# Combine step of an attention and mixture-of-experts block: an earlier first load, a second queue, other groups, another order of scales and two norms on VectorE

## The reference

```
x = layernorm(x + attention(x))            # 16 heads of 64, causal, rotary positions
x = layernorm(x + experts(x))              # 16 experts 256 -> 512 -> 256, each token uses 3
layernorm(x) = (x - mean) / sqrt(var + 1e-5)   # over the 256 numbers of a token
```

## Time and profile before

| | us |
|---|---|
| median of three runs | 1894.03 |
| the profiled execution's own time | 1896.07 |
| its span, from the first to the last instruction | 1894.1 |
| last scatter issued by POOL | 1834.14 |
| first load of the combine phase issued | 1840.62 |
| first add of POOL | 1846.17 |
| last norm of ACT ends | 1890.71 |

### The profile page before, as it was taken

One profiled execution on the slowest core, in us unless ns is written; L12 is line 12 of the kernel. 1 busy time (PEld: TensorE's weight loads), 2 busy tenths in 40 slices (PEclk: granted clock), 3 DMA queues, 4 the chain that ended last, 5 costly groups with the idle time before them and its releaser, 6 DMA issues. The chain is left out here.

```text
span 1894.1 us, 33741 instructions
## 1 busy us (share of the span) xinstructions
PE 1727.0 (91%) x9587; PEld 1288.4 (68%) x9588; DVE 1362.5 (72%) x3170; ACT 743.8 (39%) x1583; POOL 1263.0 (67%) x1086
## 2 busy tenths in 40 slices
PE   5389999999999999999999999998679999999970
PEld 4356766766666676667667666754349999999960
DVE  3358888888888888888888888865974544444435
ACT  3124445444445544444444445534442222222213
POOL 2138778767887786787778688833347777777753
PEclk8579999999999999999999999999659999999995
DMA  9856656755665676556657646613944444444447
GB/s 308 283 167 172 174 148 187 211 146 156 187 166 153 197 201 177 168 153 191 180 181 213 164 144 169 177 47 118 374 137 69 71 72 74 73 71 73 72 83 234
DMA packets 184483, 300.41 MB, mean 159 GB/s; under 512 B 22544, under 2 KB 81936, under 8 KB 184352
## 3 DMA queue, kind: packets, MB, share of 16 engines
q1 hardware_dynamic: 160784, 267.23, 47.8%
q0 software_dynamic: 21504, 30.29, 9.9%
q10 hardware_dynamic: 2064, 1.31, 0.2%
HBM read 186.84 MB, written 111.67 MB: 158 GB/s over the span
## 5 line engine op out<-in xcount | busy, mean ns | idle before, releaser
L735 ACT ACTIVATE prob<-b_ps 128x512 f32<-128x512 f32 (+3 forms) x768 | 354.6, 488 | 364.3 <-PE b_ps L572 260.7
L499 POOL TENSOR_TENSOR acc<-acc,prob 128x1024 f32<-128x1024 f32 (+1 forms) x192 | 353.1, 1839 | 6.4 <-POOL acc L499 3.2
L571 PE MATMUL b_ps<-q,k 128*128 128x512 f32 (+3 forms) x768 | 296.9, 391 | 9.7 <-DMA q<-mrow 5.2
L472 POOL TENSOR_TENSOR roped<-rot 128x512 f32<-128x512 f32 x128 | 175.0, 1367 | 184.6 <-DVE rot L858 183.8
L564 PE MATMUL a_ps<-k,q 128*128 128x512 f32 (+3 forms) x768 | 267.5, 385 | 18.6 <-DMA k<-scratch_hilo 9.7
L840 DVE CUSTOM_DVE_ANT_0 masked<-a_ps,causal 128x128 bf16<-128x128 f32 (+3 forms) x512 | 237.3, 479 | 58.8 <-PE a_ps L564 50.9
L653 PE MATMUL y_ps<-prob,v_sb 128*64 128x512 f32 (+3 forms) x1536 | 275.6, 494 | 0.0
L1573 DVE TENSOR_SCALAR hT<-h_ps,b1T 128x128 f32<-128x128 f32 x448 | 126.1, 344 | 197.4 <-PE h_ps L1489 158.4
L572 PE MATMUL b_ps<-q,k 65*128 65x512 f32 (+3 forms) x768 | 265.1, 349 | 0.0
L1463 POOL DMA_INDIRECT scratch_sum<-y,dst_i x112 | 177.8, 1587 | 95.6 <-ACT y L1538 90.8
L888 DVE RECIPROCAL inv<-inv 128x128 f32<-128x128 f32 x256 | 232.3, 929 | 8.6 <-ACT inv L776 6.2
(11 more groups left out here) (258 smaller groups left out, 2478.4 us busy)
## 6 DMA issues: line engine op xcount, KB each, us to landing
q<-scratch_hilo SPq DMA_DIRECT2D x192, 256.0 KB, 4.6
k<-scratch_hilo SPq DMA_DIRECT2D x192, 256.0 KB, 5.2
scratch_hilo<-hi SPq DMA_DIRECT2D x64, 512.0 KB, 4.2
scratch_hilo<-lo SPq DMA_DIRECT2D x64, 512.0 KB, 4.6
w_sb<-scratch_wsplit SPq DMA_DIRECT2D x32, 512.0 KB, 3.7
w<-in_L_ffn_W_dram SPq DMA_DIRECT2D x32, 512.0 KB, 9.3
wv_sb<-scratch_wsplit SPq DMA_DIRECT2D x16, 512.0 KB, 6.5
xT<-scratch_xsplit SPq DMA_DIRECT2D x6, 1024.0 KB, 6.9
```

Source lines behind the costliest of these rows:

```text
L499: nc.gpsimd.tensor_tensor(sums, old, probs(q), ALU.add).then_inc(m["sum_p"], 1)
L571: nc.tensor.matmul(out, k1[s][:, h, js], q1[s][:, h, qs], start=True, stop=False, skip_group_check=True)
L735: nc.scalar.activation(probs(q)[:, h, :], b_ps[:, h, 0:w], ACT.Exp).then_inc(exp_done[h], 1)
```

## The change

- SP, in the experts' block, waits for the last even slot's scatter (`ys_st[0]` at 16 x 56) and then issues the loads of `sum0`, one for each group, into `x1a` and `x1b`, which nothing uses by then. It enters the end of the block after that.
- ACT, at the start of the combine block, issues the loads of `sum1` into `got1`, one for each group, on its own queue.
- The groups are six: 4, 4, 8, 8, 4, 4 tiles.
- ACT then takes one square root of epsilon into a place that nothing reads yet, so that the table is loaded before the first variance is there.
- DVE's order is `moments(g)`, `scales(g)`, and then the norms that are its own.
- Tiles 27 and 31 are normalised by DVE (`tensor_scalar`), the other thirty by ACT.

```diff
+SIZES = (4, 4, 8, 8, 4, 4)
...
 def expert_phase(nc, A, dram, S):
...
+        @block.sync
+        def _(sp):
+            sp.wait_ge(ys_st[0], 16 * SLOT_TILES // SUMS)
+            sums = dram["sum0"].rearrange("(t p) d -> p t d", p=P)
+            for g, n in enumerate(SIZES):
+                t = ENDS[g] - n
+                half = S["x1a"] if t < 2 * TB else S["x1b"]
+                sp.dma_start(half[:, t % (2 * TB):t % (2 * TB) + n, :], sums[:, t:t + n, :]).then_inc(S["ld"][g], 16)
...
 def combine_phase(nc, A, dram, S, out):
-    SIZES = (4, 8, 8, 8, 4)
...
             for g in range(GROUPS):
-                for i in range(SUMS):
-                    sp.dma_start(got[i][:, rows(g), :],
-                                 dram[f"sum{i}"].rearrange("(t p) d -> p t d", p=P)[:, rows(g), :]).then_inc(ld[g], 16)
-            for g in range(GROUPS):
                 sp.wait_ge(m["c_out"], ENDS[g])
-                sp.dma_start(out_v[:, rows(g), :], got[1][:, rows(g), :]).then_inc(m["c_stored"], 16)
+                sp.dma_start(out_v[:, rows(g), :], got1[:, rows(g), :]).then_inc(m["c_stored"], 16)
...
+        def by_act(t):
+            return t < TILES - 8 or t % 4 < 3
...
-                nc.gpsimd.tensor_tensor(got[0][:, rows(g), :], got[0][:, rows(g), :], got[1][:, rows(g), :], ALU.add)\
+                nc.gpsimd.tensor_tensor(sums_of(g), sums_of(g), got1[:, rows(g), :], ALU.add)\
...
         def _(act):
+            sums = dram["sum1"].rearrange("(t p) d -> p t d", p=P)
+            for g in range(GROUPS):
+                nc.scalar.dma_start(got1[:, rows(g), :], sums[:, rows(g), :]).then_inc(ld[g], 16)
             act.wait_ge(m["c_eps"], 1)
+            nc.scalar.activation(r[:, 2, 0:1], eps[:, 0:1], ACT.Sqrt)
...
                 for t in range(ENDS[g] - SIZES[g], ENDS[g]):
+                    if by_act(t):
+                        nc.scalar.activation(got1[:, t, :], token_rows(S, t), ACT.Identity, bias=r[:, 4, t:t + 1],
+                                             scale=r[:, 3, t:t + 1]).then_inc(m["c_out"], 1)
...
-            moments(0)
+            def normalize(g):
+                for t in range(ENDS[g] - SIZES[g], ENDS[g]):
+                    if not by_act(t):
+                        dve.wait_ge(m["c_rs"], g + 1)
+                        V.tensor_scalar(got1[:, t, :], token_rows(S, t), r[:, 3, t:t + 1], r[:, 4, t:t + 1], ALU.mult,
+                                        ALU.add).then_inc(m["c_out"], 1)
             for g in range(GROUPS):
-                if g + 1 < GROUPS:
-                    moments(g + 1)
+                moments(g)
                 scales(g)
+                normalize(g)
```

More of the change, by code:

```diff
@@ L912 @@
 AHEAD = 4
+SIZES = (4, 4, 8, 8, 4, 4)
+ENDS = [sum(SIZES[:g + 1]) for g in range(len(SIZES))]
 SUMS = 2
@@ L1595, in combine_phase @@
 def combine_phase(nc, A, dram, S, out):
-    SIZES = (4, 8, 8, 8, 4)
-    ENDS = [sum(SIZES[:g + 1]) for g in range(len(SIZES))]
     GROUPS = len(SIZES)
@@ L1602, in sb @@
             return ctx.enter_context(nc.sbuf_tensor(name, shape, dt))
-        got = [sb(f"got{i}", [P, TILES, D], F32) for i in range(2)]
+        got1 = sb("got1", [P, TILES, D], F32)
         stats = sb("stats2", [P, TILES, 6], F32)
@@ L1610, in combine_phase @@
         m = {k: ctx.enter_context(nc.semaphore(k)) for k in names}
-        ld = [ctx.enter_context(nc.semaphore(f"got_ld{g}")) for g in range(GROUPS)]
+        ld = S["ld"]
         block = ctx.enter_context(nc.Block())
@@ L1620, in _, with sums_of @@
             for g in range(GROUPS):
-                for i in range(SUMS):
-                    sp.dma_start(got[i][:, rows(g), :],
-                                 dram[f"sum{i}"].rearrange("(t p) d -> p t d", p=P)[:, rows(g), :]).then_inc(ld[g], 16)
-            for g in range(GROUPS):
                 sp.wait_ge(m["c_out"], ENDS[g])
-                sp.dma_start(out_v[:, rows(g), :], got[1][:, rows(g), :]).then_inc(m["c_stored"], 16)
+                sp.dma_start(out_v[:, rows(g), :], got1[:, rows(g), :]).then_inc(m["c_stored"], 16)
             sp.wait_ge(m["c_stored"], 16 * GROUPS)
+        def sums_of(g):
+            first, end = ENDS[g] - SIZES[g], ENDS[g]
+            return (S["x1a"] if first < 2 * TB else S["x1b"])[:, first % (2 * TB):first % (2 * TB) + end - first, :]
+        def by_act(t):
+            return t < TILES - 8 or t % 4 < 3
         @block.gpsimd
@@ L1644, in _ @@
                 for t in range(ENDS[g] - SIZES[g], ENDS[g]):
-                    nc.scalar.activation(got[1][:, t, :], got[0][:, t, :], ACT.Identity, bias=r[:, 4, t:t + 1],
-                                         scale=r[:, 3, t:t + 1]).then_inc(m["c_out"], 1)
+                    if by_act(t):
+                        nc.scalar.activation(got1[:, t, :], token_rows(S, t), ACT.Identity, bias=r[:, 4, t:t + 1],
+                                             scale=r[:, 3, t:t + 1]).then_inc(m["c_out"], 1)
         @block.vector
@@ L1663, in moments @@
                 for t in range(ENDS[g] - SIZES[g], ENDS[g]):
-                    ins = V.bn_stats(stats[:, t, :], got[0][:, t, :])
+                    ins = V.bn_stats(stats[:, t, :], token_rows(S, t))
                 link(ins)
@@ L1701, in post_ln_block @@
         S.update(zeros=sb("zeros", [P, D], F32), sums_in=ctx.enter_context(nc.semaphore("sums_in")))
+        S["ld"] = [ctx.enter_context(nc.semaphore(f"got_ld{g}")) for g in range(len(SIZES))]
         with ExitStack() as inner:
```

## The result

The changed kernel is slower: 1900.62 us (median of six runs, 1898.39 to 1903.62) against 1894.39 for the kernel before (six runs, 1891.88 to 1897.43), a ratio of 1.0031 with a 95% interval of 1.0020 to 1.0042, so 3.8 to 8.0 us more. The forecast was +4.4, to 1898.4, with a range of 1889.2 to 1902.0.

A forecast was written before the change was run, and what follows sets the result against it. ACT's chain of norms bounds the end, its start held by data and by DVE waiting behind POOL. Last norm 1895.1 against 1890.7 gives +4.4 us, applied to the median 1894.03: 1898.4, range 1889.2 to 1902.0.

The forecast's parts named there:

- the narrower 1896.5 to 1900: Range for the main forecast of +4.4 us alone, allowing 0.7 us error in group 2's landing and small pause errors.
- SP's held issues: Early sum0 loads: each issue held until all but 1.6 to 1.8 MB ahead has moved; sixth ends at 1843.4.
- The drain: SP's drain at the experts' block's end: 1.4 us after its last issue, 1844.8, so ACT's first load at 1845.1.
- Landing and adds: Combine loads and POOL: groups 0, 1, 2 landed at 1850.6, 1853.6, 1856.6; adds without a gap from 1856.6 to 1870.3.
- What the early load brings POOL: End of POOL's adds in the combine block: the early load brings it only 1.2 us.
- ACT behind its own issues: ACT's stream: six issues held until 1855.4, then table load 1.28 and small root 0.30, ready at 1857.0.
- The rival in which ACT is not held: ACT's sum1 issues are not held, group 0 normalised early, group 1's scales caught by adds: +0.9 us, 1894.9; chance 0.20.
- The wait behind POOL: Group 0's scales: DVE's two-input instructions wait for POOL's running add, one passing per add's end; first norm at 1870.5.
- From there: ACT's norms and pauses for all 32 tiles, from the first norm at 1870.5 to the last norm's end at 1895.1.
- The one with no wait behind POOL (-7.6): DVE's scales do not wait for POOL's adds: first norm at 1858.5, -7.6 us, 1886.4; chance 0.06.
- The rival of the drain that waits for landing: SP's drain waits for 4 MB to land: barrier 1850.9, adds until 1873.2, +7.3 us, 1901.3; chance 0.08.
- The turns that a DMA engine takes between loaded queues: Combine loads: SP's and ACT's queues share the flow evenly; otherwise group 0 at about 1852.3 and the same sum.

The follow-up runs named there:

- after_again: The changed kernel run again unaltered, beside the kernel before: median 1899.02 us against 1895.72, ratio 1.0019.
- a1_psum: The changed kernel with the small tiles of the scales split between PSUM and SBUF: ratio 0.9957 to the kernel before.
- a6_no_early: The changed kernel without the early load; SP issues sum0's six loads at the start of the combine block: ratio 1.0014 to the kernel before.
- a4_act_three: The changed kernel with ACT issuing only three loads of sum1 and SP the other three: ratio 1.0005 to the kernel before.
- a2_table_first: The changed kernel with ACT's small square root, and so its table load, ahead of its six issues: ratio 1.0015 to the kernel before.
- c1_best: The changed kernel with split scales, four early loads, three ACT loads, table first, root and moments ahead, three tiles on DVE: ratio 0.9950 to the kernel before.
- c2_front_loaded: The changed kernel with split scales, groups 4, 4, 8, 8, 8, two early loads, other loads by SP, last eight tiles shared: 1882.86 us, ratio 0.9930 to before.

## Why the prediction was right

The forecast was +4.4 us, and the two profiles differ by 4.3. The medians differ by 6.2 and 3.3 in the two sets of runs. The first time, 1900.62, lies in the range of 1889.2 to 1902.0, but above the narrower 1896.5 to 1900 that was given for this mechanism. The chances were 0.41 for no change that can be told and 0.40 for slower, so slower was not held to be likelier than no change. The steps can be followed in the profile after, one by one.

- **SP's held issues.** Forecast: the sixth ends at 1843.4; it ended at 1837.46 + 5.80 = 1843.26. The rule read from the earlier trace rows, that an issue is held until all but 1.6 to 1.8 MB ahead of it has moved, held for a queue that had six loads in place of ten. That it fits within 0.14 us is luck in part: counted from the last scatter the issue ended after 9.3 us, as forecast, but after 9.5 to 10.5 in the profiles of the five other kernels or executions with the same early load (after_again 9.9, a1_psum 10.5).
- **The drain** was the wrong step: forecast 1.4 us after the issue, from the earlier trace rows; it started at 1843.3, at once, and took 120 ns while the last of SP's data landed only at 1853.3. ACT's first issue came at 1843.68, not 1845.1. As the prediction said, the end hardly depends on the barrier: after_again had it 0.6 us later and the same stretch.
- **Landing and adds.** Group 0 forecast at 1850.6, its add started at 1850.96; group 2 at 1856.6, measured 1856.45; POOL's end 1870.3, measured 1869.99. Two errors cancel in these. With ACT's issue where it was, the same working gives group 0 at 1849.2, but the load landed at 1850.9, 7.2 us after its issue. And the flow was 383 to 388 GB/s from 1844 to 1852 where the sum has 349, so that by my estimate from these stretches 6 MB had moved by 1855, yet group 2 was known as landed only at 1856.3: the 0.6 us for that was too small here.
- **What the early load brings POOL.** Forecast 1.2 us. POOL ended 1.3 us earlier after the last scatter than before (36.0 against 37.3), but a6_no_early has that without the early load. The size was right and the cause wrong.
- **ACT behind its own issues.** Forecast free at 1855.4, measured 1854.86; the first root ended at 1856.57, 0.7 earlier than forecast, and still 0.1 us after the start of the add that caught it. The rival in which ACT is not held would have had the table load before 1852; it came at 1854.88.
- **The wait behind POOL.** Forecast one instruction for each end of an add, first norm at 1870.5; measured 1870.24. a1_psum shows what it depends on. One reading was short: the old order had three such waits, not two, since L1675 of group 1 also took 1.8 us, to the end of an add at 1869.2 (row below). One detail was left open and is settled: L1697, a `tensor_scalar` with one input in SBUF, waits as well (2.27 us here, 4.41 and 4.42 in a4_act_three and a2_table_first).
- **From there** 24.6 us to the last norm were forecast (1870.5 to 1895.1), 24.6 measured (1870.24 to 1894.87). DVE's norm of a tile, estimated at 0.34, takes 0.41.

The third wait in the kernel before, from its chain of waits (start us, us, what):

```profile
1867.37 1.86 DVE r L1675
```

The rival that I gave 0.20, ACT not held, is refuted by the 4.69, 3.45 and 1.45 us of its issues. The one with no wait behind POOL (-7.6) named the size of what a1_psum then found when the wait was taken away (-6.8), so its working was right and its condition wrong. The rival of the drain that waits for landing fell with the 120 ns row.

The turns that a DMA engine takes between loaded queues, by the Trainium skill, "DMA: Bandwidth & Descriptors", section "Queues, rings and completion order", now have a trace that bears on them, and it agrees. While both queues were loaded, SP's last MB landed between 1847.9 and 1853.3, and ACT's second half MB between 1850.9 and 1853.5: about 0.19 MB per us each, by my estimate from the landings. The table load has 1.28 us here as in the kernel before. The 2.66 us that the Trainium skill, "ScalarE: Activation LUTs", section "What ACT_TABLE_LOAD costs", gives for it with its drain again don't appear: the small root starts at 1856.18, 1.30 us after the load's start.

## What to carry to other kernels

Before work is moved earlier, ask what the later user does in the gaps that go away: here DVE's small instructions got past POOL's adds one at each end of an add, and otherwise only in the time in which POOL waited for data. A chain of tiny instructions with operands in SBUF is priced here not by its own length (0.17 us each) but by the adds it meets, one for each, and one of two operands in PSUM takes an instruction off that list. And an early load should not be so large that its issues are held, for then the block's end and all that is queued behind wait too: six early loads put the next block's first issue 9.7 us after the last scatter, while four in c1_best and two in c2_front_loaded left the block's end at 6.6 to 6.7 us, where it was without any (6.5).

## What the runs showed of the hardware that I had not expected

A `tensor_scalar` of 128 x 4 with one input in SBUF waited for the whole of a POOL add (4.42 us), while a reciprocal, `bn_stats` and `bn_aggr` never did in these traces; with its input and output in PSUM it took 0.17 us under a running add.

The loads moved at 347 to 350 GB/s for most of the time in the kernel before but at 384 to 387 in a6_no_early from 1850 to 1866. These are stretches of a6_no_early, columns as in the earlier trace rows:

```profile
1850.00:1852.00 2.00, 0.00 (x0) 0.00 (x0) 1.14 (x7) 0.00 (x0) 1.42 (x1) 0.50 1.09 387
...
1864.00:1866.00 2.00, 0.00 (x0) 0.00 (x0) 1.97 (x2) 0.00 (x0) 2.00 (x2) 0.50 1.09 385
```

In the changed kernel it was 383 to 388 from 1844 to 1852, with both queues loaded, and 348 to 349 from 1854 to 1860, when all of SP's loads had landed. Two queues would explain it, but c2_front_loaded reached 385 and 386 with SP's queue alone. What sets the two rates stays open.
